# Moving one of five gated projection products of a group from VectorE to ScalarE

## The reference, cut to what matters

```python
# L0_ffn, per batch: H, E, DH, K = 8, 5, 64, 3
ss_g = sigmoid(x @ Ws) * top3_mask        # gates of k and v, one number per token, head, expert
sd_g = sigmoid(x @ Wd) * top3_mask        # gates of q
q = einsum('bthed,bthe->bhtd', (x @ Wq ).reshape(b, t, H, E, DH), sd_g)   # k and v alike, with ss_g
attn = softmax(q * scale @ k)             # 8 heads, 256 x 256
out  = attn @ v                           # and from it the output projection, masked by top 3
```

## Time and profile before

| | |
|---|---|
| median of the runs | 717.81 us |
| the profiled execution's own time | 718.16 us |
| its span in the profile | 716.3 us |
| mean granted clock of PE, share of full speed | 0.885 |
| PE busy | 583.4 us (81%) |
| DVE busy | 507.1 us (71%) |
| ACT busy | 346.6 us (48%) |
| POOL busy | 372.9 us (52%) |
| L808, products on DVE | 120 of them, 683 ns each |

### The profile page before, as it was taken

How to read it: one execution, slowest core, us unless ns; L and a number is a source line. 1 busy time by engine, 2 the same in 40 slices (tenths; PEclk the granted TensorE clock), 3 DMA queues, 4 the chain that set the end, 5 groups by cost and what they waited for, 6 DMA issues and landing times. The chain is left out here.

```text
span 716.3 us, 15684 instructions
## 1 busy us (share of the span) xinstructions
PE 583.4 (81%) x5739; PEld 392.3 (55%) x5739; DVE 507.1 (71%) x1069; ACT 346.6 (48%) x750; POOL 372.9 (52%) x322
## 2 busy tenths in 40 slices
PE   5399865779859858976747879999999999878896
PEld 5277622245335425434634346677677667666785
DVE  4936899867964982895695677776767776667653
ACT  2333200042173136218542567877887886624554
POOL 5513345564744745574547456666775666632221
PEclk9999997758957985995556899999999999999998
DMA  6410000020000000000021000000000000000000
GB/s 186 110 39 31 30 30 0 0 89 1 1 1 1 0 0 0 0 0 0 30 63 56 1 1 2 2 2 2 2 3 1 3 2 2 1 2 1 2 9 26
DMA packets 14175, 13.12 MB, mean 18 GB/s; under 512 B 3120, under 2 KB 11936, under 8 KB 14112
## 3 DMA queue, kind: packets, MB, share of 16 engines
q1 hardware_dynamic: 14112, 12.25, 5.8%
HBM read 11.72 MB, written 0.52 MB: 17 GB/s over the span
## 5 line engine op out<-in xcount | busy, mean ns | idle before, releaser
L1465 POOL TENSOR_TENSOR attn<-work,attn 128x512 f16<-128x512 f32 (+1 forms) x96 | 142.0, 1481 | 85.7 <-ACT attn L1272 85.6
L808 DVE TENSOR_TENSOR work<-banks,gatev 128x512 f32<-128x512 f32 x120 | 79.3, 683 | 16.4 <-PE banks L513 15.9
L1365 DVE TENSOR_REDUCE nmax<-banks 128x2 bf16<-128x1024 f32 x64 | 77.9, 1217 | 3.0 <-PE banks L1117 1.9
L511 PE MATMUL banks<-weights,xbTh 128*128 128x512 f16 x120 | 51.2, 426 | 28.2 <-DVE work L808 26.8
L1269 ACT ACTIVATE work<-banks,maskbias 128x512 f32<-128x512 f32 x64 | 44.2, 691 | 41.5 <-PE banks L1143 41.5
L2053 PE MATMUL banks<-ident,work 128*128 128x128 f32 x276 | 52.4, 327 | 8.6 <-DVE work L2253 3.0
L943 POOL TENSOR_TENSOR work<-work 128x512 f32<-128x512 f32 x24 | 30.5, 1269 | 43.5 <-DVE work L808 41.4
L1161 PE MATMUL banks<-work,attn 128*128 128x65 f16 x512 | 51.7, 196 | 1.6 <-POOL attn L1465 1.0
L1161 PEld LDWEIGHTS banks<-work,attn 128*128 128x128 f16 x512 | 48.2, 99 | 8.0 <-POOL attn L1465 4.5
L1162 PE MATMUL banks<-work,attn 128*128 128x65 f16 x512 | 51.8, 196 | 0.0
L1163 PE MATMUL banks<-work,attn 128*128 128x65 f16 x512 | 51.7, 196 | 0.0
(11 more groups left out here) (327 smaller groups left out, 1895.0 us busy)
## 6 DMA issues: line engine op xcount, KB each, us to landing
stage<-in_L_ffn_w SPq DMA_DIRECT2D x8, 512.0 KB, 4.2
stage<-in_L_ffn_Wkv SPq DMA_DIRECT2D x4, 640.0 KB, 4.1
stage<-in_L_ffn_Wq SPq DMA_DIRECT2D x2, 640.0 KB, 5.1
xt<-in_x SPq DMA_DIRECT2D x1, 512.0 KB, 4.4
ct<-in_ctx SPq DMA_DIRECT2D x1, 512.0 KB, 5.6
wo<-in_L_xattn_Wo SPq DMA_DIRECT2D x1, 512.0 KB
stage<-in_L_xattn_Wv SPq DMA_DIRECT2D x1, 512.0 KB, 3.7
stage<-in_L_xattn_Wq SPq DMA_DIRECT2D x1, 512.0 KB, 3.5
```

Source lines behind the costliest of these rows:

```text
L511: pe.matmul(o, xh, wh, start=True, stop=False)
L808: dve.tensor_tensor(heads8(m.prod[:, k, e, :]), heads8(bank_pj[c % 2][:, :]), wide(g, DH1), ALU.mult).then_inc(s.prod_ready, 1)
L1365: dve.tensor_reduce(m.nmax[:, p % 2, i, :], banks[:, 6:8, :], AX.X, ALU.max, negate=True).then_inc(s.c_max_done, 1)
L1465: pool.tensor_tensor(m.Pl[:, p % 2, kts, :], m.Pf[:, kts, :], m.Ph[:, p % 2, kts, :], ALU.subtract).then_inc(s.c_P_lo, 1)
```

## The change

In the loop, chunk e1 of groups 1 to 5 is no longer multiplied on DVE. ACT does it in eight activations of 128x64, one for each head: Copy with the token's gate as the scale, from the PSUM bank into `prod`. The first batch's chunks and group 0 stay as they were. PE's wait before e3 (which reuses e1's bank) is now for ACT. POOL adds e0 + e2 first and e1 after it.

```diff
+        ACT_GROUPS = SUMS - 1
+        def on_act(b, c):
+            return not isinstance(b, int) and c >= E1 and c % E1 == 1
             def project(b, c):
-                if c >= 2 or not isinstance(b, int) or b > 0:
+                if c >= 2 and on_act(b, c - 2):
+                    pe.wait_ge(s.prod_act, b * ACT_GROUPS + (c - 2) // E1)
+                elif c >= 2 or not isinstance(b, int) or b > 0:
                     pe.wait_ge(s.prod_ready, b * X1 + (c - 1))
...
+            def gate_chunk(b, c, group):
+                part, i, e = chunk(c)
+                k, sel = c // E1 % 2, G1 if part == 0 else 0
+                act.wait_ge(s.prod_free, group - 1)
+                act.wait_ge(s.pj_ready, b * X1 + (c + 1))
+                act.sem_inc(s.chunk_begun, 1)
+                for h in range(H1):
+                    r, at = slice(DH1 * h, DH1 * h + DH1), sel + h * E1 + e
+                    ins = act.activation(m.prod[:, k, e, r], bank_pj[c % 2][:, r], ACT.Copy, scale=m.gatev[:, b * I + i, at:at + 1])
+                ins.then_inc(s.prod_act, 1)
...
                 if more:
+                    for c in sum(chunks_of(h), []):
+                        if on_act(b + 1, c):
+                            gate_chunk(b + 1, c, SUMS + b * GROUPS + c // E1)
                     for k in turns_of(h):
                         high_qk(b + 1, k)
...
             def gate_products(b, c, group):
+                if on_act(b, c):
+                    return
...
-                dve.tensor_tensor(..., ALU.mult).then_inc(s.prod_ready, 1)
+                dve.tensor_tensor(..., ALU.mult).then_inc(s.prod_ready, 2 if on_act(b, c + 1) else 1)
...
-                ch.link(pool.tensor_tensor(acc, pr[:, 0, :], pr[:, 1, :], ALU.add))
-                pool.wait_ge(s.prod_ready, b * X1 + (k * E1 + 3))
-                ch.link(pool.tensor_tensor(acc, acc, pr[:, 2, :], ALU.add))
+                if on_act(b, k * E1 + 1):
+                    pool.wait_ge(s.prod_ready, b * X1 + (k * E1 + 3))
+                    ch.link(pool.tensor_tensor(acc, pr[:, 0, :], pr[:, 2, :], ALU.add))
+                    pool.wait_ge(s.prod_act, b * ACT_GROUPS + k)
+                    ch.link(pool.tensor_tensor(acc, acc, pr[:, 1, :], ALU.add))
+                else:
...
```

More of the change, by code:

```diff
@@ L365, in build @@
         s.prod_free = sem("prod_free")
+        s.prod_act = sem("prod_act")
+        s.chunk_begun = sem("chunk_begun")
         s.acc_ready = sem("acc_ready")
@@ L671, in act_b @@
             act.sem_inc(s.exp_done, RING)
+            act.sem_inc(s.prod_act, ACT_GROUPS)
+            act.wait_ge(s.gate_ready, 1)
+            def gate_chunk(b, c, group):
[8 more added lines that the diff above has]
+                ins.then_inc(s.prod_act, 1)
             def high_qk(b, k):
@@ L807, in gate_products @@
                 g = m.gatev[:, b * I + i, sel:sel + G1].rearrange("p (h e) -> p h e", h=H1)[:, :, e]
-                dve.tensor_tensor(heads8(m.prod[:, k, e, :]), heads8(bank_pj[c % 2][:, :]), wide(g, DH1), ALU.mult).then_inc(s.prod_ready, 1)
+                dve.tensor_tensor(heads8(m.prod[:, k, e, :]), heads8(bank_pj[c % 2][:, :]), wide(g, DH1), ALU.mult)\
+                    .then_inc(s.prod_ready, 2 if on_act(b, c + 1) else 1)
                 if e == E1 - 1:
@@ L942, in sums @@
                         pool.wait_ge(s.v1lo_ready, (b - 1) * I + (k - 4 + 1))
-                ch.link(pool.tensor_tensor(acc, pr[:, 0, :], pr[:, 1, :], ALU.add))
-                pool.wait_ge(s.prod_ready, b * X1 + (k * E1 + 3))
-                ch.link(pool.tensor_tensor(acc, acc, pr[:, 2, :], ALU.add))
+                if on_act(b, k * E1 + 1):
[4 more added lines that the diff above has]
+                else:
+                    ch.link(pool.tensor_tensor(acc, pr[:, 0, :], pr[:, 1, :], ALU.add))
+                    pool.wait_ge(s.prod_ready, b * X1 + (k * E1 + 3))
+                    ch.link(pool.tensor_tensor(acc, acc, pr[:, 2, :], ALU.add))
                 pool.wait_ge(s.pair_ready, b * SUMS + (k + 1))
```

## The result

| | before | after |
|---|---|---|
| median of the runs | 719.28 us (716.2 to 721.22, 4 runs) | 731.11 us (730.34 to 732.75, 4 runs) |
| ratio | | 1.0169, 95% interval 1.0135 to 1.0204 |
| profiled execution, span | 718.16, 716.3 us | 730.65, 728.8 us |
| mean granted clock of PE | 0.885 | 0.883 |

The change makes the kernel slower by 11.8 us, 1.7%. The forecast was 723 us, and its range ended at 729. (The median of before is over four runs here; over three it was 717.81.)

A forecast was written before the change was run, and what follows sets the result against it. The prediction took bank hold time in the two-bank ring, from projection start to product end, as what counts. Step terms summed to +1.8 us a turn, 5.5 over three turns: 723 us against the median, range 715 to 729.

The forecast's parts named there:

- on time for each of these: In the two-bank ring, DVE's remaining products would not delay the links of each step's period; nothing charged.
- step 7: First ring step with an ACT product: ACT's activations stand behind its exponentials, delaying e3 and the next e0; +0.86 us.
- step 8: Ring step from e0 to the next e0: 5.36 us against 4.72, +0.64 us.
- step 9: Ring step with two turnings on PE: 5.85 us against 5.44, +0.41 us.
- step 10: Ring step with one turning on PE: 5.42 us against 5.51, -0.09 us.
- step 11: Last of these ring steps, up to its turning: 4.98 us against 4.77, +0.21 us.
- DVE is freer now: -0.2: After the last turning, ACT copies the turned k and DVE takes the low half just behind the pair; -0.2 us.
- the prediction's other estimate, 2.0: Eight ACT activations priced from the Trainium skill's figures: 2.0 us instead of 1.87, adding 2 us to the sum.
- ACT's hold: ACT's eight activations hold e1's bank, 3.0 us from e1's projection to e3, so PE waits; sum +1.8 us a turn.
- DVE's relief wins: Rival: ACT's product fits under PE's 2.36 us between e1 and e3; each step loses up to 0.60; 709 to 716, chance 0.1.
- PE's clock falls in the ring: Rival: new waits at e3 lower PE's clock, 1.8 us a step; 729 to 745 us, chance 0.12.
- The bank is held longer: Rival: ACT's queue waits, register steps and write to `prod` make each link 0.2 us longer; 727 us, chance 0.2.

The follow-up runs named there:

- e1: Not a run: the chunk in each ring step whose product the change moves from DVE to ACT in groups 1 to 5; no time of its own.
- e3: Not a run: a later chunk of the same ring step, whose projection on PE reuses the PSUM bank of e1; no time of its own.

## Why the prediction was wrong

- **The step that failed**: "DVE has one product fewer and is on time for each of these; POOL's adds take 3 x 1.27 and the gaps between the earlier trace rows, some 4.4 us, inside the period, and start later only by waiting for e2", for which nothing was charged. Only POOL's own length was looked at. The adds do stay within the period, and POOL is as busy as before; what they cost is that DVE's pair waits under the middle one, and so DVE is late: PE waits for it 1.69 and 1.96 us at e2 of steps 10 and 11. It wasn't on time there before either (0.97 and 1.05). The order alone costs 3.67 us a turn.
- **The steps, measured** from e0 to e0: step 7 +0.62 (forecast +0.86), step 8 +0.49 (+0.64), step 9 +0.31 (+0.41), step 10 +0.72 (-0.09), step 11 +0.92 (+0.21), and from the last turning to the last low half +0.78 (-0.2). Steps 7 to 9 make +1.42 for +1.91. Steps 10, 11 and the tail make +2.42 for -0.08, and the pairs there are longer by 0.80 (1.49 for 0.69), 0.92 (1.68 for 0.76) and 0.78 (1.47 for 0.69), 2.50 in all. That is the miss: 2.5 us a turn too little there, 0.5 too much in steps 7 to 9, and in all 3.84 measured for 1.83 forecast.
- **"DVE is freer now: -0.2"** had the wrong sign for the same reason: the last pair is on the way to the low half, and it takes 1.47 us.
- **ACT's product was priced well**: 332 ns for one (forecast 320), eight in 1.75 us (forecast 1.87, with 1.75 as its low end; the prediction's other estimate, 2.0, is further off). From e1 to e3 2.83 us (242.20 to 245.03) for 3.0. The wait at e3 ended by ACT came in steps 7 to 9 alone, 0.65, 0.22 and 0.32 us, where the forecast named five of 0.6 to 1.1.
- **The size of ACT's hold**, forecast +1.8 us a turn: +1.25 where no pair is stretched (pair added before e1), +1.66 with POOL's old order, where four pairs still take 0.83 to 0.93. That the latter kernel's +5.8 us is near the forecast's +5.5 is so in part by that stretch.
- **DVE's relief wins** (0.1): false, and not only for the length of the activations. With one activation in place of eight the ring is as long as before. "Each step loses up to 0.60" took a busy engine for the bound, where the bound is a chain that e1's product is no part of.
- **PE's clock falls in the ring** (0.12): it stayed at 1.00, also with waits of 1.69 and 1.96 us.
- **The bank is held longer** (0.2): its 727 lies nearer to the 731 measured than the forecast's 723, but by luck. The links were shorter than priced, not longer.

The sign of steps 10 and 11 could have been found in the trace of before. The six pairs there took 0.69 us four times, and 0.77 and 0.76 where POOL's middle add (ended 242.96 and 253.70) was over a little after the pair's start (242.74 and 253.49): a row in a group, 12% long, was the sign of the collision, and POOL's move shifted that add by the wait for e2.

## What to carry over

When an edit reorders work on one engine, check not only whether it still fits, but which instructions of the other engine it will newly lie over; look for same-shaped instructions of unequal length and see what ran beside the longest. A reordering that only spares one engine a wait can cost more on another than the change it serves. And before work is taken from a full engine, follow the round trips: an engine can be full while the chain that sets the period runs past the instruction that is taken away.

## What the runs showed of the hardware

A DVE add (128x512, f32) with two SBUF operands that began under a POOL add of two SBUF operands ended 0.55 us after POOL's, whenever it had begun: 253.62 to 254.17, 260.35 to 260.90, 266.46 to 267.01, and 252.41 to 252.96 in the kernel before with POOL's new order. Alone it takes 0.69. DVE's mask products, which read other tensors than the pair, were stretched under a POOL add too (2.58 us for three that take 1.88 alone). POOL can be the one that waits: its add at 265.45, begun while DVE's mask products ran, took 1.50 us for 1.27. A DVE instruction of the same size with one operand in PSUM is not touched: 0.67 us at 249.05 (below), in the midst of POOL's add of 248.61 to 249.87.

```profile
249.05 0.67 DVE L869 TENSOR_TENSOR attn<-banks,attn 128x512 f16<-128x512 f32 x1
```

The Trainium skill, SBUF — State Buffer, section Who interferes with whom, says that a VectorE instruction with two SBUF inputs contends with a GpSimd instruction that reads SBUF, that the contention is an exclusive lock on a shared pair of ports and the order of issue decides which of the two blocks, and that with at most one SBUF input, outside of some faster modes, VectorE doesn't contend. The traces agree on who waits for whom, in each of the three points, with the numbers above; that it is the ports, no run here shows.
